# A new order of all stages in a metaformer block: experts in half units, eight of them on pair 0's four PSUM banks

## What is computed

```python
x = x + conv(layernorm_over_height(x))      # shapes as the reference has them
t = tokens of x                             # 4096 tokens of 64 features
x = x + experts(layernorm(t))
```

## Time and profile before

| what | value |
|---|---|
| runs | 228.48, 228.86 and 229.04 us |
| profiled execution | span 227.4 us from its first to its last instruction; its own time is not listed apart, and the median of the runs is 1.46 us above the span |
| TensorE (PE) | busy 206.7 us, 91% of the span |
| VectorE (DVE) | busy 123.8 us, 54% |
| ScalarE (ACT) | busy 128.1 us, 56% |
| GpSimd (POOL) | busy 47.0 us, 21% |
| TensorE's mean granted clock | 0.981 of full speed |

### The profile page before, as it was taken

The page is one execution under the profiler, slowest core; times in us unless marked ns, Lnnn a source line. Parts: engine busy times, 40 slices in busy tenths (PEclk is TensorE's granted clock), DMA queues, the critical chain, the costliest instruction groups (busy, mean ns, idle before and its releaser), DMA issues.

```text
span 227.4 us, 4913 instructions
## 1 busy us (share of the span) xinstructions
PE 206.7 (91%) x2096; PEld 113.6 (50%) x2096; DVE 123.8 (54%) x232; ACT 128.1 (56%) x207; POOL 47.0 (21%) x50
## 2 busy tenths in 40 slices
PE   7699788999976898988899799999999999999993
PEld 3395667566334577963524244444444444444430
DVE  0582055659949977999731633554334553334555
ACT  2256942035338553669685387666786666786640
POOL 5560393040069992030400000000000000000000
PEclk9979999999999999999699999999999999999998
DMA  6990000000000000000005953260804508063001
GB/s 219 294 265 14 0 3 6 3 0 7 0 0 4 0 3 0 3 0 0 3 0 164 220 128 69 82 151 0 184 3 108 122 4 184 0 150 84 0 0 46
DMA packets 6596, 14.35 MB, mean 63 GB/s; under 512 B 2736, under 2 KB 4144, under 8 KB 5680
## 3 DMA queue, kind: packets, MB, share of 16 engines
q1 hardware_dynamic: 6576, 14.06, 24.7%
HBM read 12.87 MB, written 1.18 MB: 62 GB/s over the span
## 4 chain that ended last, share of the span: by engine, by line
PE 68%; ACT 9%; DMA 7%; POOL 6%; DVE 6%; SPq 1%; issue 1%; POOLq 1%; DVEq 0%
PE psum L710 22%; PE psum L694 21%; PE psum L538 7%; DMA xs<-in_x 3%; DMA wide<-gate_store 2%; PE psum L512 2%; POOL place L920 2%; ACT place L747 2%; PE psum L634 2%; PE psum L548 2%; PE psum L424 2%; POOL place L926 2%; ACT hid L861 1%; POOL place L919 1%; PE psum L557 1%
## 5 line engine op out<-in xcount | busy, mean ns | idle before, releaser
L694 PE MATMUL psum<-tok,w1s 128*64 128x512 f16 x512 | 60.8, 383 | 1.3 <-ACT hid L861 0.8
L1160 DVE SCALAR_TENSOR_TENSOR term<-psum,sm,wide 128x512 f32<-128x512 f32 x32 | 24.0, 750 | 62.1 <-PE psum L710 51.6
L861 ACT ACTIVATE hid<-psum,b1p 128x512 f32<-128x512 f32 x64 | 38.2, 701 | 16.7 <-PE psum L694 16.3
L694 PEld LDWEIGHTS psum<-tok,w1s 128*64 128x64 f16 x512 | 28.7, 110 | 35.9 <-issue 9.1
L861 ACT ACTIVATE w1f<-psum,b1p 128x512 f32<-128x512 f32 x32 | 19.6, 688 | 17.1 <-PE psum L694 17.0
L710 PE MATMUL psum<-hid,w 128*64 128x512 f32 x128 | 28.9, 593 | 0.0
L1165 DVE TENSOR_TENSOR x<-x,term 128x512 f32<-128x512 f32 x32 | 22.1, 692 | 1.1
L861 ACT ACTIVATE w1g<-psum,b1p 128x512 f32<-128x512 f32 x32 | 19.7, 714 | 0.2
L710 PEld LDWEIGHTS psum<-hid,w 128*64 128x64 f32 x128 | 9.1, 137 | 15.1 <-issue 9.4
L710 PE MATMUL psum<-w1g,w 128*64 128x512 f32 x64 | 15.1, 594 | 1.4 <-DVE term L1160 1.4
L538 PE MATMUL psum<-h_pad,tap_bd 64*64 64x512 f32 x144 | 15.9, 589 | 0.0
(11 more groups left out here) (147 smaller groups left out, 295.4 us busy)
## 6 DMA issues: line engine op xcount, KB each, us to landing
wide<-gate_store SPq DMA_DIRECT2D x14, 512.0 KB, 6.4
xs<-in_x SPq DMA_DIRECT2D x2, 512.0 KB, 5.6
w1f<-in_W SPq DMA_DIRECT2D x2, 512.0 KB, 10.0
block_out<-x SPq DMA_DIRECT2D x4, 256.0 KB, 6.4
wide<-gate_store SPq DMA_DIRECT2D x2, 384.0 KB, 5.1
c<-const SPq DMA_DIRECT2D x1, 548.5 KB, 4.4
hid<-in_W1T SPq DMA_DIRECT2D x1, 512.0 KB, 10.3
w<-in_W SPq DMA_DIRECT2D x1, 512.0 KB, 11.8
```

Of the source, the lines that this page charges most:

```text
L694: mm = pe.matmul(h_bank(n)[side * H:(side + 1) * H, :], w1s[:, part, e, k * P + side * H:k * P + (side + 1) * H], tok[:, pair, half, b, :] ...
L861: act.activation(hid_of[u % 4][:, t, :], h_bank(n), ACT.Gelu, bias=b1p[:, e * KT + k:e * KT + k + 1]).then_inc(gelu_ready, 1)
L1160: dve.scalar_tensor_tensor(term[:, u % 2, :], y_bank(u), b2t[:, e:e + 1], gate_b[part][:, e % (E // 2), :], ALU.add, ALU.mult).then_inc(te ...
```

## The change

It gives every stage a new turn on every engine, and each half of each expert unit (one `k`) a turn of its own. Eight units instead of four use the two early banks; the `y` banks are now the two of slot(0, 0), so the first eight units use pair 0's four banks alone, and later tiles have pair 0's slot(0, 1) and both slots of pair 1. `down` of the first unit waits for pair 0's gates only, and `up` of the ninth unit for both pairs'. SP stores pair 1's gates behind four loads and the first output. ScalarE's first instruction is a GELU of one zeroed column, and VectorE's `coef_rest` becomes a stage, `coefficients`. POOL's order becomes `weights_of_first`, `join(0)`, `high(0)`, `join(1)`, `high(1)`, `low_part(0)`, `low_part(1)`.

```diff
 TURN = {
-    "router_weights": (3, 3), "keep_router_weights": (5, 5), "weights_of_first": (1, 1), "dct_over_h": (1, 2),
-    "square_columns": (1, 2), "dct_over_w": (4, 7), "windows": (5, 9), "conv_in": (6, 11), "keep_dw": (3, 7),
-    "keep_xd": (4, 9), "gelu_in": (6, 10), "norm_columns": (1, 2), "places": (8, 13), "keep_xt": (8, 12),
-    "join": (2, 3), "high": (4, 5), "gram_matrices": (10, 16), "gram_times_w": (12, 18), "norms": (14, 20),
-    "mask_gram": (3, 7), "taps": (17, 23), "logits": (15, 22), "products": (4, 8), "keep_tk": (11, 14),
-    "inverse_norms": (5, 10), "scale_logits": (6, 12), "norms_of_k": (19, 24), "softmax_in": (9, 13),
-    "softmax_out": (11, 15), "gelu_depthwise": (13, 17), "gelu_out": (15, 21), "conv_out": (21, 29),
-    "project": (25, 30), "exponent": (16, 20), "heads": (26, 31), "times_wv": (27, 32), "keep_y": (18, 22),
-    "low": (28, 34), "mask_mix": (14, 17), "keep_yt": (19, 23), "to_frequencies": (33, 38),
-    "inverse_over_kh": (35, 40), "keep_back": (24, 27), "keep_half": (25, 28), "square_tokens": (26, 31),
-    "mix_branches": (16, 18), "inverse_over_kw": (36, 41), "high_part": (29, 92), "tokens": (37, 43),
-    "residual": (19, 22), "norm_tokens": (21, 24), "keep_tokens": (30, 93), "features": (42, 92), "low_part": (6, 7),
-    "router": (39, 91), "route": (23, 25), "gates_to_rows": (101, 102), "shares": (26, 27), "biases": (20, 20),
-    "tanh_gap": (91, 94), "keep_gates": (101, 102),
+    "dct_over_h": (0, 1), "dct_over_w": (2, 7), "router_weights": (3, 3), "windows": (4, 9),
+    "conv_in": (5, 11), "places": (6, 13), "gram_matrices": (8, 15), "gram_times_w": (10, 17),
+    "norms": (12, 20), "logits": (14, 21), "taps": (16, 22), "norms_of_k": (18, 24), "conv_out": (19, 26),
+    "project": (23, 29), "heads": (25, 30), "times_wv": (27, 31), "low": (28, 33), "to_frequencies": (32, 36),
+    "inverse_over_kh": (34, 38), "inverse_over_kw": (35, 40), "tokens": (37, 41), "router": (39, 43),
+    "features": (42, 55), "gates_to_rows": (45, 74), "norm_columns": (0, 1), "mask_gram": (2, 7),
+    "products": (3, 9), "coefficients": (4, 4), "biases": (5, 5), "inverse_norms": (6, 11),
+    "scale_logits": (8, 13), "softmax_in": (10, 14), "softmax_out": (12, 16), "mask_mix": (15, 18),
+    "mix_branches": (17, 19), "residual": (20, 22), "norm_tokens": (21, 25), "route": (23, 29),
+    "shares": (24, 31), "square_columns": (0, 1), "keep_dw": (2, 7), "keep_router_weights": (3, 3),
+    "keep_xd": (4, 8), "gelu_in": (5, 10), "keep_xt": (6, 11), "keep_tk": (9, 13), "gelu_depthwise": (12, 16),
+    "gelu_out": (14, 20), "exponent": (15, 19), "keep_y": (17, 21), "keep_yt": (18, 22),
+    "keep_back": (23, 25), "keep_half": (24, 27), "square_tokens": (26, 29), "high_part": (28, 37),
+    "keep_tokens": (30, 40), "tanh_gap": (31, 47), "keep_gates": (33, 51), "weights_of_first": (0, 0),
+    "join": (1, 3), "high": (2, 4), "low_part": (5, 6),
 }
 
 UNITS = STEPS * E
-ROUNDS = UNITS // 2
-AHEAD = 2
-
-
-def round_turn(r):
-
-    return 100 + 10 * (r + 1)
-
-
-def in_turn(stages, experts=None):
+KEPT = 4
+EARLY = 8
+EXPERT_TURN = {
+    "up": [
+        44, 46, 48, 50, 52, 54, 57, 59, 61, 63, 65, 67, 69, 71, 73, 76, 78, 79, 80, 82, 83, 84, 85, 92, 93,
...
+    "down": [
+        47, 49, 51, 53, 56, 58, 60, 62, 64, 66, 68, 70, 72, 75, 77, 81, 86, 87, 88, 89, 90, 91, 99, 100,
...
+    "gelu": [
+        32, 34, 35, 36, 38, 39, 41, 42, 43, 44, 45, 46, 48, 49, 50, 52, 53, 54, 55, 56, 57, 58, 59, 60, 61,
...
+    "add": [
+        26, 27, 28, 30, 32, 33, 34, 35, 36, 37, 38, 39, 40, 41, 42, 43, 44, 45, 46, 47, 48, 49, 50, 51, 52,
...
+def in_turn(stages, experts):
 
     turns = [(TURN[f.__name__][p], f, (p,)) for f in stages for p in range(PAIRS)]
-    if experts:
-        turns += [(round_turn(r), experts, (r,)) for r in range(-AHEAD, ROUNDS)]
+    for f in experts:
+        parts = 1 if f.__name__ == "add" else 2
+        turns += [(EXPERT_TURN[f.__name__][parts * u + part], f, (u, part)[:parts]) for u in range(UNITS) for part in range(parts)]
     return [(f, args) for _, f, args in sorted(turns, key=lambda t: t[0])]
...
-        h_late = h_early + [bank(slot(1, 1), 0), bank(slot(1, 1), 1), bank(slot(1, 0), 1), bank(slot(0, 0), 0)]
-        y_banks = [bank(slot(0, 0), 1), bank(slot(1, 0), 0)]
+        h_late = h_early + [bank(slot(1, n), j) for n in (1, 0) for j in range(2)]
+        y_banks = [bank(slot(0, 0), 1), bank(slot(0, 0), 0)]
         TILES = B2 * KT
-        EARLY = 2 * AHEAD
 
         def h_bank(n):
 
             early = EARLY * TILES
-            return h_early[n % len(h_early)] if n < early else h_late[n % len(h_late)]
+            return h_early[n % len(h_early)] if n < early else h_late[(n - early) % len(h_late)]
...
             store_gates(0)
-            load_gates(0)
-            load_gates(1)
-            store_gates(1)
-            for n in range(2, 2 * STEPS):
+            for n in range(2 * STEPS):
+                if n == STEPS:
+                    store_gates(1)
                 load_gates(n)
-                if n % 2:
+                if n % 2 and n > 1:
                     store_out(n // 2 - 1)
...
-            def up(u):
+            def up(u, k):
 
                 i, e = divmod(u, E)
                 pair, half = divmod(i, 2)
-                if u == 0:
+                if u == 0 and k == 0:
                     pe.wait_ge(bias_ready, 1)
                     pe.wait_ge(w1_ready, 1)
-                if e == 0:
+                if e == 0 and k == 0:
                     pe.wait_ge(tok_ready, 2 * (pair + 1))
-                if u == EARLY:
+                if u == EARLY and k == 0:
                     pe.wait_ge(gates_ready, PAIRS)
-                for t in range(TILES):
-                    k, b = divmod(t, B2)
-                    n = TILES * u + t
+                for b in range(B2):
+                    n = TILES * u + B2 * k + b
...
-            def down(u):
+            def down(u, k):
 
                 e = u % E
-                if u == 1:
-                    pe.wait_ge(gates_ready, PAIRS)
+                if u == 0 and k == 0:
+                    pe.wait_ge(gates_ready, 1)
                 before = last_in(y_bank, u)
-                if before >= 0:
+                if before >= 0 and k == 0:
                     pe.wait_ge(term_done, before + 1)
-                for k in range(KT):
-                    pe.wait_ge(gelu_ready, TILES * u + B2 * (k + 1))
-                    for b in range(B2):
-                        mm = pe.matmul(y_bank(u)[b * H:(b + 1) * H, :], w2[:, e * KT + k, :], hid_of[u % 4][:, B2 * k + b, :],
-                                       start=k == 0, stop=k == KT - 1)
-                mm.then_inc(w2_done, 1)
-
-            def experts(r):
-
-                if r >= 0:
-                    down(2 * r)
-                    down(2 * r + 1)
-                for u in (2 * (r + AHEAD), 2 * (r + AHEAD) + 1):
-                    if u < UNITS:
-                        up(u)
+                pe.wait_ge(gelu_ready, TILES * u + B2 * (k + 1))
+                for b in range(B2):
+                    mm = pe.matmul(y_bank(u)[b * H:(b + 1) * H, :], w2[:, e * KT + k, :], hid_of[u % KEPT][:, B2 * k + b, :],
+                                   start=k == 0, stop=k == KT - 1)
+                if k == KT - 1:
+                    mm.then_inc(w2_done, 1)
...
+            def gelu(u, k):
+                if u >= KEPT and k == 0:
+                    act.wait_ge(w2_done, u - KEPT + 1)
...
+            act.wait_ge(still_zero, 1)
+            act.activation(first_gelu[:, :], still[:, 0:1], ACT.Gelu)
...
-            dve.wait_ge(weights_in, 16)
-            dve.tensor_scalar(coef_rest[:, :], coef, -1.0, 1.0, ALU.mult, ALU.add).then_inc(coef_ready, 1)
+            def coefficients(p):
+
+                if p:
+                    return
+                dve.wait_ge(weights_in, 16)
+                dve.tensor_scalar(coef_rest[:, :], coef, -1.0, 1.0, ALU.mult, ALU.add).then_inc(coef_ready, 1)
 
```

More of the change, by code:

```diff
@@ L235, in metaformer @@
         still = sb("still", [P, CHUNK], F16)
+        first_gelu = sb("first_gelu", [P, 1])
         gate_rows = sb("gate_rows", [P, PAIRS, P])
@@ L725, in _ @@
                       inverse_over_kw, tokens, router, features, gates_to_rows)
-            for stage, args in in_turn(stages, experts):
+            for stage, args in in_turn(stages, (up, down)):
                 stage(*args)
@@ L843, in keep_gates @@
                 act.copy(gate_rows[:, p, :], slot(p, 0)[:, P:2 * P]).then_inc(gates_ready, 1)
[L846 to L859 removed]
+            def gelu(u, k):
+                e = u % E
+                if u >= KEPT and k == 0:
+                    act.wait_ge(w2_done, u - KEPT + 1)
+                for b in range(B2):
+                    n = TILES * u + B2 * k + b
                     act.wait_ge(w1_done, n + 1)
[L861 removed]
+                    act.activation(hid_of[u % KEPT][:, B2 * k + b, :], h_bank(n), ACT.Gelu,
```

(17 more changed lines are left out.)

14 lines of the change are left out of this document (2 added, 12 removed), and 6 rows, old and new, of the table EXPERT_TURN.

## The result

The changed kernel takes 222.53 us (median of four runs, 222.11 to 223.97) beside 228.67 us for the kernel before (228.29 to 229.04): a ratio of 0.9724, 95% interval 0.9684 to 0.9764. The forecast was 222.0. The profiled execution has a span of 219.7 us and a time of 222.11.

The account below looks back on a forecast made before the run. TensorE's holes in front of 110.1 us of expert work bound the kernel. Span 227.4 + 1.2 (later first `up`) - 8.1 (experts) = 220.5, plus 1.46 around it gives 222.0 us; range 217 to 226.

Parts of the forecast that it names:

- VectorE and POOL: Ahead of `norms_of_k(1)`: POOL's `high(0)` and `join(1)` hold VectorE's softmax and inverse root; without loss it starts 4.65 us earlier.
- The first rival: Ahead of `norms_of_k(1)`: VectorE and POOL hardly meet, the inverse root isn't held at each step; 4.65 less, 217.3; chance 0.10.
- The start: Up to 46.9 us: `conv_in(0)` starts where it did, holes shrink from 3.0 to 0.55 us, `taps(0)` starts 2.45 earlier.
- the last term: Around the span: the runs' median lies 1.46 us above the profiled execution's span, so 220.5 becomes 222.0.
- my second rival: Between `taps(1)` and `norms_of_k(1)`: TensorE's clock falls, 2.7 us of work takes twice that; 224.7; chance 0.20.
- The forecast's own mechanism: Ahead of `norms_of_k(1)`: VectorE's SBUF instructions stand until POOL's running one ends, so it starts 2.3 us later, at 66.85.
- The experts: From the first `up` to the end of the last `down`: 113.8 us where it was 121.9, 8.1 less.
- the two tile banks and the switches: In the experts: banks don't serialise (otherwise 8.8 us more), and 57 switches between `up` and `down` cost 0, at most 1.0.
- The gates: In the first eight units: pair 0's gates come 0.5 late; with ScalarE's copies TensorE waits some 2 us.
- my own last sign of being wrong: In the first eight units: the prediction is wrong if TensorE waits for `term` or the gates there.
- The slower rival: First `up` to unit 8: the clock falls, half of 27.5 us at 1.2 GHz, 13.8 more, 235.8; chance 0.08.

Follow-up runs that it names:

- `join(1)` first: The changed kernel with POOL's old order alone, `join(1)` ahead of `high(0)`: 217.58 us, ratio 0.9503 to the kernel before.
- `high(0)` held back: The changed kernel, POOL's order as changed, but `high(0)` waits until VectorE has written pair 1's norms: 221.73 us, ratio 0.9665.
- the matmuls of zeros: The changed kernel with six clock-holding matmuls of zeros ahead of each half of `project(0)`: 221.72 us, ratio 0.967.
- the split `high(0)`: The changed kernel with `high(0)` cut in two on POOL, its first image before `join(1)`, its second behind it: 217.17 us.

## Why the prediction was right, and where it was not

**VectorE and POOL** was the step on which most hung, and it held. I had put 3.7 us on the inverse root; `inverse_norms(1)` took 8.1 us (51.38 to 59.49), against 4.3: 3.8. The last multiplies of `softmax_in(0)` and `softmax_out(0)` lost 1.0 each, for 1.1 forecast. All of it together was priced at 4.65 at `norms_of_k(1)`; with it taken away by `join(1)` first that started 5.9 earlier, 0.9 of them from the clock in `project(0)`, so 5.0; with `high(0)` held back it started 5.7 earlier. The first rival, that the two hardly meet, is refuted by the same rows. The rule behind it was too wide: I had every VectorE instruction with SBUF operands only stand. Those with two SBUF operands stood, and so did the `coefficients` step (2.96 us behind POOL's 4.13 at 27.25) and the first step of the root (0.98), but TENSOR_REDUCE and RECIPROCAL (0.68 and 0.35 inside `join(1)`'s 2.62) ran on. The Trainium skill, "SBUF — State Buffer", section "SBUF: two separate sides", has it that GpSimd shares a pair of ports with a VectorE instruction that runs in a 2-port perf mode, or that has two SBUF inputs while GpSimd's reads SBUF, and that whichever starts first holds the pair for its whole length. The multiplies that stood and the sums that ran on agree with it; whether the `coefficients` step and the first step of the root, with one SBUF input each, ran in such a mode no trace shows.

**The start** held relative to itself: `conv_in(0)` to `taps(0)` 16.45 us, forecast 16.5. But `conv_in(0)` came at 18.08, not 20.05: `x1` arrived 1.0 us earlier and `dct_over_h(1)` took 2.05, not the 3.55 of the earlier trace rows, at full clock. That is no work of the change: with the old order of the conv stages and the new experts `conv_in(0)` came at 18.49, with the changed order and the matmuls of zeros at 19.91, and in all other executions profiled after the prediction between 17.89 and 18.64. I took the one execution before for typical. The other half of the same mistake is the last term: I added 1.46 for what lies around the span, and every later run of every kernel lies 2.1 to 2.6 above its own span. By that, the profiled execution of the kernel before, at 227.4, was some 0.9 longer than its median run.

**The clock between `taps(1)` and `norms_of_k(1)`** was my second rival, at 0.20, and it is what happened in both profiled executions of the changed kernel. Its price was put at 2.7; the first `up` lost 1.5 in the one and about 2.6 in the other. (The execution without the first GELU shows the case without a fall: first `up` 83.3 behind `conv_in(0)`, 82.2 without the load's 1.1, forecast 82.8; measured 83.7 and 84.8.) The forecast's own mechanism and this rival were no alternatives; they hold together, and I should have put the fall's chance much higher, as TensorE's idle time there was in my own working.

**The experts** came as forecast: 114.0 for 113.8, halves every 0.86 us, 13.00 of 13.00 us busy in 117 to 130, so the two tile banks and the switches cost nothing that shows. The gates were 1.1 late instead of 0.5; by my own last sign of being wrong, a wait for the gates in the first eight units, this part was too hopeful. The slower rival, a clock that falls in the two-bank phase, did not come: 1.00 from 101.8 on. It did come, for some 4 us, in the profile of the split `high(0)`. The Trainium skill's rule in "TensorE: Matmul & The Clock Gate", section "A second HAM failure mode: psum-queue depth-cycling", would have made it 235.8 in my reckoning. It speaks of banks in turn with short idle times between the groups; here, but for the 1.1 us at the gates, the groups had no holes between them, so this trace neither bears the rule out nor tests it.

So that the sum came within 0.5 us is in part luck, by terms that cancel: the start 2.0 early; from `conv_in(0)` to the first `up` 0.9 late (1.5 for the fall, 0.6 early in the rest); the experts 0.2 late; and 0.9 more around the span.

## What to carry to other kernels

Ahead of a reorder, lay VectorE's and GpSimd's queues side by side and look where chains of short two-operand SBUF instructions on the one fall on long instructions of the other: each link can then cost a whole foreign instruction, as four of eight did here, and one swapped stage was worth more than half of what the whole experts' part brought. A gain at the front of a kernel counts only if the next engine in the chain can take it; follow it stage by stage to the last stage. Before using a profile as the base of a sum, see from other runs how far its own start lies from the usual.

## What was not expected of the hardware

A VectorE instruction that comes just as a POOL instruction ends goes first and holds POOL's next one (1.67 and 1.62 us for 1.27). There it started 0.17 and 0.20 us ahead of that next one; in the earlier trace rows a multiply that came 0.14 us behind POOL's start was held itself. So which engine loses turns on some 0.3 us of timing. The trace of the kernel before had such rows as well (POOL's second instruction of `high(0)`, at 68.13, took 1.75 us behind a multiply at 68.05), and the prediction did not use them. And with the same order the clock may or may not fall at the same place: `norms_of_k(1)` took 2.57 and 3.73 us in two executions of the changed kernel, and 1.98 in the one without the first GELU, each time after two waits of 1.65 to 1.67 us.
